# A twelve-layer perceiver: who normalises x at seven layer borders, and when two self attentions' weights are loaded

## Chip, cores and metric

The kernel runs on one core of one Trainium2 chip. The metric is device time in microseconds of one launch; a time "before" is the median of three runs. The profile is one execution more, with its own time. Engines: TensorE (PE in the rows, PEld its weight loads), VectorE (DVE), ScalarE (ACT), GpSimd (POOL) and SyncE (SP), which issues the loads.

## What is computed

x is 64 sequences of 32 tokens of 256 values: 2048 tokens. Twelve layers follow one another, each x = x + layer(layernorm(x)): four blocks L0 to L3, each of a cross attention to a context of 64 x 257 x 256, a self attention over the 32 tokens of a sequence, and an FFN (two of them with a router over experts).

```
x = x + L0_xattn(layernorm(x), ctx, mask, ...)
x = x + L0_attn(layernorm(x), Wq, Wk, Wv, Wo, ...)
x = x + L0_ffn(layernorm(x), ...)
...
x = x + L3_xattn(layernorm(x), ctx, ctx, ...)
x = x + L3_attn(layernorm(x), Wq, Wk, Wv, Wo, bo)
x = x + L3_ffn(layernorm(x), ...)
```

layernorm subtracts the mean of a token's 256 values and divides by the root of their variance + 1e-5. Because a layer adds to x token by token, the last token's sum closes a layer, and the next one's normalisation hangs on it.

## The kernel before

x stays in SBUF as 16 row blocks of 128 tokens (`K.x[:, i, :]`), four blocks to a group. Every layer is a function with one program for each engine; each engine runs its layers one after the other, and semaphores are all that ties the engines together. `barrier` is the wait for the last x of the layer ahead. POOL's program for a norm stands ahead of its `barrier`, so POOL may start on the next layer's norm as soon as it is through with its own work and a group's statistics are there. The other engines wait at the barrier first.

The names that matter. `follow` makes the statistics (mean and variance, `K.mv`) of row block i - 1 on VectorE while block i is added, so the statistics of a layer's last block come last of all. `Norm` (L203) and `NormParts` (L286) are the two forms of the norm, over four groups g = 0 to 3:

- `pool`: the reciprocal root of the variance, `K.rs`, by an add (L245, L330) and a pow (L247, L332); in `NormParts` also `K.nb`, minus mean times root (L333, L335), which ScalarE needs as its bias.
- `apply`: xn = (x - mean) * rs, one instruction of 128x256 for a row block. In `Norm` VectorE does all 16 (L258). In `NormParts` VectorE does two of a group (L343) and ScalarE two (L360).
- `pe`: eight transposes a group, of xn against the identity, into two PSUM banks (L234, L322). All 32 stand ahead of the layer's own products in TensorE's program.
- `evict`: VectorE and ScalarE copy a bank each to `K.xT`. In `NormParts` ScalarE makes an upper part and VectorE subtracts for a lower one (L350), because the products there are made of three partial ones.

`Norm` is used by L0 self attention, L0 FFN, L1 cross attention, L1 FFN, L2 cross attention and L3 cross attention; `NormParts` by L1 self attention, L2 self attention, L2 FFN and L3 self attention.

In L0 self attention (`l0_attn`) POOL clears four `qk` and ten `v` tiles (L1175) behind its norm, and then takes, for each of 16 row blocks, a pow of 128x32 (L1183) for the norm of q and k. The first product is L189 on `l0a_wqk`. Its weights are loaded behind the barrier, 1.3 MB.

In L3 self attention (`wide_attn` with bias False) the four weights are loaded behind the barrier as well. ScalarE and VectorE split each into an upper and a lower part (`upper`, `lower`, L1361); the first four halves, those of q and k, stand between the norm's groups in the two engines' programs.

In L3 cross attention (`l3_xattn`) 64 batches run through `ticks`. For each, POOL subtracts for the context's lower part (L3944) and scales one of four blocks of probabilities (L3976). SP loads the context of a batch, four buffers ahead.

L0 FFN and L1 FFN collect their sums in DRAM and load x back at their end, so at the border behind them all of x comes at about one time.

## Times and profile before

| | us |
|---|---|
| median of three runs | 3618.52 |
| lowest, highest | 3613.38, 3622.97 |
| the profiled execution | 3626.44 |
| its span in the profile | 3624.7 |
| TensorE busy | 3287.8 (91%) |
| VectorE busy | 2199.3 (61%) |
| ScalarE busy | 1308.9 (36%) |
| POOL busy | 1138.8 (31%) |

Shares are of the span. The mean granted clock of TensorE was 0.945 of full speed. A row of the timeline gives start, length, engine, line, operation, what is written from what, and how many instructions of one kind stand together; square brackets hold the idle time of the engine ahead of it and who ended it. Times count from the start of the span.

### The profile page before, as it was taken

To read this page: it belongs to the slowest core of one execution; us is meant where nothing else is said; L and a number is where in the kernel's file an instruction comes from. 1 tells how busy PE (TensorE), PEld (TensorE's weight loads), DVE (VectorE), ACT (ScalarE), POOL (GpSimd) and SP (SyncE) were. 2 spreads that over 40 slices of the span, in tenths; PEclk is the share of its full clock that TensorE was granted. 3 is DMA by queue.
4 is the path that set the end of the run, shared out by engine and by line. 5 is a ranking of instruction groups with operands and counts; after the bars stand their busy time and mean duration, and the time that the engine had idled before them with its cause. 6 is when DMAs were issued, how large, how long until landed. Compare 5 with 4: busy or idle time off the path is not lost.

```text
span 3624.7 us, 95053 instructions
## 1 busy us (share of the span) xinstructions
PE 3287.8 (91%) x40252; PEld 2747.2 (76%) x40252; DVE 2199.3 (61%) x5264; ACT 1308.9 (36%) x3221; POOL 1138.8 (31%) x1717
## 2 busy tenths in 40 slices
PE   7989659988997979999999779979999999998996
PEld 5866547547986758888888667778888878887894
DVE  5757643356665156666666577755444458887557
ACT  5643101333211224444444443323222236665221
POOL 6767124122003334333333343300000025554102
PEclk9999769999996979999999999989999999999997
DMA  5620348541003321111111100012112211111000
GB/s 161 199 68 4 107 164 263 158 147 49 3 19 113 89 76 54 48 48 48 48 48 42 57 2 3 3 48 90 58 60 92 64 42 49 51 50 63 3 3 27
DMA packets 211335, 246.66 MB, mean 68 GB/s; under 512 B 19460, under 2 KB 191232, under 8 KB 207968
## 3 DMA queue, kind: packets, MB, share of 16 engines
q1 hardware_dynamic: 203424, 230.34, 20.2%
q0 software_dynamic: 7488, 10.23, 1.6%
q8 instruction: 320, 5.24, 0.6%
q14 instruction: 103, 0.84, 0.1%
HBM read 221.46 MB, written 18.61 MB: 66 GB/s over the span
## 4 chain that ended last, share of the span: by engine, by line
PE 77%; DVE 12%; issue 4%; POOL 3%; ACT 3%; DMA 1%; SPq 0%; ACTq 0%; POOLq 0%; DVEq 0%
PE psum L189 46%; PE psum L3648 11%; PE psum L983 2%; PE psum L3898 2%; PE psum L955 2%; PE psum L3107 1%; PE psum L3208 1%; PE psum L3176 1%; PE psum L3888 1%; PE psum L968 1%; DVE l2a_ss L1651 1%; POOL l0a_ms L1183 1%; DVE g_xn L258 1%; PE psum L3117 1%; DVE g_xn L1658 1%
## 5 line engine op out<-in xcount | busy, mean ns | idle before, releaser
L245 POOL TENSOR_SCALAR g_rs<-g_mv 128x4 f32<-128x4 f32 x24 | 5.1, 213 | 773.9 <-DVE g_mv L378 773.4
L3648 PE MATMUL psum<-l2f_hhi,l2f_whi 128*128 128x512 f32 x512 | 199.3, 389 | 0.0
L3648 PE MATMUL psum<-l2f_hlo,l2f_whi 128*128 128x512 f32 x512 | 199.2, 389 | 0.0
L3648 PE MATMUL psum<-l2f_hhi,l2f_wlo 128*128 128x512 f32 x512 | 199.2, 389 | 0.0
L189 PE MATMUL psum<-l2x_kT,l2x_Qp 128*128 128x257 f32 x768 | 179.0, 382 | 2.7 <-ACT g_xn L3531 2.7
L3702 DVE CAST l2f_hhi<-l2f_tmp 128x512 fp32r<-128x512 f32 x96 | 41.0, 427 | 201.7 <-ACT l2f_tmp L3765 200.6
L189 PEld LDWEIGHTS psum<-l2x_kT,l2x_Qp 128*128 128x128 f32 x768 | 141.9, 191 | 21.9 <-issue 3.3
L389 DVE TENSOR_TENSOR g_x<-g_x,psum 128x256 f32<-128x256 f32 x128 | 53.1, 416 | 129.0 <-PE psum L189 125.8
L3765 ACT ACTIVATE l2f_tmp<-psum,g_cols 128x512 f32<-128x512 f32 x64 | 44.2, 690 | 240.2 <-PE psum L3648 240.2
L3531 ACT ACTIVATE g_xn<-psum,l2x_sm 128x257 f32<-128x257 f32 x192 | 89.0, 473 | 90.5 <-DVE l2x_sm L3437 90.5
L4095 ACT ACTIVATE l3x_P<-psum,l3x_sm 128x257 f32<-128x257 f32 x256 | 117.8, 480 | 2.8 <-DVE l3x_sm L4017 2.6
L3648 PEld LDWEIGHTS psum<-l2f_hlo,l2f_whi 128*128 128x128 f32 x512 | 96.1, 188 | 20.2
L3648 PEld LDWEIGHTS psum<-l2f_hhi,l2f_wlo 128*128 128x128 f32 x512 | 96.1, 188 | 20.0
L3648 PEld LDWEIGHTS psum<-l2f_hhi,l2f_whi 128*128 128x128 f32 x512 | 96.1, 188 | 19.8
L200 ACT ACTIVATE l2x_Pc<-psum 128x384 f32<-128x384 f32 x128 | 61.2, 494 | 134.6 <-PE psum L189 134.5
L189 PE MATMUL psum<-g_xn_parts,l2x_tokhi 128*128 128x384 f32 x256 | 93.7, 366 | 3.5 <-DVE l2x_PTlo L3460 1.7
L3446 DVE TENSOR_SCALAR g_xn<-g_xn,l2x_sm 128x257 f32<-128x257 f32 x192 | 91.6, 532 | 2.3
L3460 DVE SCALAR_TENSOR_TENSOR l2x_PTlo<-psum,l1f_next_rk,g_xn_parts 128x384 fp32r<-128x384 f32 x128 | 73.1, 613 | 32.1 <-ACT g_xn_parts L3541 31.3
L1592 POOL TENSOR_TENSOR l2a_ss<-l2a_ss,g_negh 128x32 f32<-128x32 f32 x16 | 90.8, 5673 | 1.3
L3107 PE MATMUL psum<-l1f_next_GG,l2x_cT 128*128 128x257 f32 x256 | 81.6, 401 | 8.4 <-ACT l2x_Qp L200 5.6
L1183 POOL TENSOR_TENSOR l0a_ms<-l0a_ms,g_negh 128x32 f32<-128x32 f32 x16 | 86.8, 5428 | 1.3
L189 PE MATMUL psum<-l2x_PTlo,l2x_tokhi 128*128 128x384 f32 x256 | 86.4, 337 | 0.0
(877 smaller groups left out, 10770.2 us busy)
## 6 DMA issues: line engine op xcount, KB each, us to landing
l2f_raw<-L2f_h SPq DMA_DIRECT2D x64, 512.0 KB, 3.4
l0f_w<-L0f_w SPq DMA_DIRECT2D x23, 1024.0 KB, 8.0
l0x_ctxT<-ctxT SPq DMA_DIRECT2D x64, 257.0 KB, 2.8
l1x_ctxT<-ctxT SPq DMA_DIRECT2D x64, 257.0 KB, 6.3
l0x_ctok<-ctx SPq DMA_DIRECT2D x64, 256.0 KB, 3.1
l1x_ctok<-ctx SPq DMA_DIRECT2D x64, 256.0 KB
l2x_cT<-ctxT SPq DMA_DIRECT2D x64, 256.0 KB, 2.8
l2x_tok<-ctx SPq DMA_DIRECT2D x128, 128.0 KB, 2.9
```

The lines of the kernel that those rows point to most:

```text
L189: ins = e.matmul(out, lhsT, rhs, start=start and n == 0, stop=stop and n == len(pairs) - 1, skip_group_check=skip)
L955: t = e.matmul(self.s_bank[par][32 * j:32 * j + 32, ch * self.nk:(ch + 1) * self.nk], qT[r, ch, 32 * j:32 * j + 32], kT[r, ch, j, :], star ...
L983: t = e.matmul(self.o_bank[j][par * hd:(par + 1) * hd, ch * 32:ch * 32 + 32], v[s, b * hd:(b + 1) * hd], PT[s, par * nch + ch, :], start=n ...
L1183: e.tensor_tensor(m, m, K.negh[:, 0:32], ALU.pow).then_inc(*rs_ok.up())
L1592: e.tensor_tensor(f, f, K.negh[:, 0:32], ALU.pow).then_inc(*rs_ok.up())
L3107: e.matmul(z[:, 0:257], a[:, 1, k], GG[:, 1, :], start=True, stop=False, skip_group_check=True)
L3446: t = e.tensor_scalar(P[b % 3][:, n, :], P[b % 3][:, n, :], m(4)[:, n:n + 1], None, ALU.mult)
L3460: e.scalar_tensor_tensor(out=lo[:, kt, :], in0=banks.of(("T", b, kt))[:, 0:384], scalar=rk[:, b, kt:kt + 1], in1=hi[:, kt, :], op0=ALU.mul ...
L3531: t = e.activation(P[k][:, n, :], bank[n][:, 0:257], ACT.Exp, bias=sm[:, k, 2, n:n + 1], scale=0.125, accum_out=sm[:, k, 3, n:n + 1])
L3648: t = e.matmul(z, a, b, start=c == 0 and u == 0, stop=c == 7 and u == 2)
L3898: t = e.transpose(z[:, r * 128:(r + 1) * 128], P[b % 3][:, r, kt * 128:(kt + 1) * 128], ident[:])
L4095: e.activation(P[k][:, r, :], bank[r][:, 0:257], ACT.Exp, bias=sm[:, k, 1, r:r + 1], accum_out=sm[:, k, 2, r:r + 1]).then_inc(*exps.up())
```

## The change

`Norm` and `NormParts` get an argument `early`. With it, POOL also normalises: all four blocks of groups 0, 1 and 2, each right behind the group's root. It can do so while the layer ahead still runs, since this stands ahead of its barrier. In `Norm` POOL does two blocks of group 3 as well and ScalarE the other two, for which POOL now makes `K.nb`; in `NormParts` group 3 stays with VectorE and ScalarE. VectorE has no `apply` in `Norm` any more.

`early` is on for L0 self attention, L0 FFN, L1 FFN and L3 cross attention (`Norm`), and for L3 self attention (`NormParts`). L1 and L2 cross attention have it off; there POOL does two blocks of each group and ScalarE two, behind the statistics as before. L1 self attention, L2 self attention and L2 FFN are as before.

The weights of L0 self attention are loaded in L0 cross attention (ahead of batch 32), those for q and k of L3 self attention in L3 cross attention (ahead of batch 8). The split of the latter is done there too: ScalarE's four copies at batches 36 to 39, POOL's four subtractions at batches 40 to 43, each at the end of a tick. v and o are loaded and split as before.

Three waits are also eased: the first products of L0 self attention and of L2 cross attention wait for group 2 and not for all four, and the routers' first products for group 1.

```diff
 class Norm:
-    def __init__(self, K, second=None, first=False):
+    def __init__(self, K, second=None, early=True):
...
+    def by_act(self, g):
+        return not self.early or g == 3
+
+    def normed(self, w, g):
+        if self.early:
+            w.wait_ge(self.xn_pool.at(14 if g == 3 else 4 * g + 4))
+        else:
+            w.wait_ge(self.xn_pool.at(2 * g + 2))
+        if self.by_act(g):
+            w.wait_ge(self.xn_act.at(2 if self.early else 2 * g + 2))
...
     def pool(self, e, w):
...
-            e.tensor_tensor(K.rs[:, sl], K.rs[:, sl], K.negh[:, 0:4], ALU.pow).then_inc(*self.rs.up())
+            t = e.tensor_tensor(K.rs[:, sl], K.rs[:, sl], K.negh[:, 0:4], ALU.pow)
+            if self.by_act(g):
+                t.then_inc(*step.up())
+                e.tensor_scalar(K.nb[:, sl], K.mv[:, sl, 0], -1.0, None, ALU.mult).then_inc(*step.up())
+                w.wait_ge(step.now())
+                e.tensor_tensor(K.nb[:, sl], K.nb[:, sl], K.rs[:, sl], ALU.mult).then_inc(*self.rs.up())
+            else:
+                t.then_inc(*self.rs.up())
+            w.wait_ge(self.rs.now())
+            for i in range(4 * g, 4 * g + (2 if self.by_act(g) else 4)):
+                e.tensor_scalar(K.xn[:, i, :], K.x[:, i, :], K.mv[:, i, 0:1], K.rs[:, i:i + 1], ALU.subtract,
+                                ALU.mult).then_inc(*self.xn_pool.up())
...
 class NormParts:
...
     def pool(self, e, w):
...
             e.tensor_tensor(K.nb[:, sl], K.nb[:, sl], K.rs[:, sl], ALU.mult).then_inc(*self.rs.up())
+            if self.ahead(g):
+                for i in range(4 * g, 4 * g + 4):
+                    e.tensor_scalar(K.xn[:, i, :], K.x[:, i, :], K.mv[:, i, 0:1], K.rs[:, i:i + 1], ALU.subtract,
+                                    ALU.mult).then_inc(*self.xn_pool.up())
...
 def l0_xattn(K):
...
             for b in range(4, 64):
+                if b == 32:
+                    K.first.sp(e)
                 fetch(b)
...
 def l0_attn(K):
...
-            load_rows(e, wt, wqk, A["L0a_qk"])
-            load_rows(e, wt, wv, A["L0a_v"])
-            load_rows(e, wt, wo, A["L0a_o"])
...
-                norm.ready(w, i // 4)
-                w.wait_ge(mark["w"])
+                norm.ready(w, max(i // 4, min(i + 2, 3)))
+                w.wait_ge(K.first.w_in.at(0))
...
-            norm.all_ready(w)
...
 def wide_attn(K, pre, bias, eps, scale, keep, brow_name):
...
+        ahead, own = (None, "qkvo") if bias else (K.last, "vo")
...
-            for u in range(6):
+            for u in range(4 if ahead else 0, 6):
...
+        def in_norm(split):
+            return (lambda g: None) if ahead else split
...
-            norm.dve(e, w, lambda g: lower(e, w, g))
+            norm.dve(e, w, in_norm(lambda g: lower(e, w, g)))
...
 class Router:
...
-            self.norm.ready(w, i // 4)
+            self.norm.ready(w, max(i // 4, 1))
...
 def l3_xattn(K):
...
             for b in range(64):
+                if b == 8:
+                    K.last.sp(e)
...
+            def weights(b):
+                if 40 <= b < 44:
+                    K.last.pool(e, b - 40)
...
+            def weights(b):
+                if 36 <= b < 40:
+                    K.last.act(e, b - 36)
```

How instructions stand on three of the places. The names: g_rs, g_nb, g_xn and g_x are the tiles `K.rs`, `K.nb`, `K.xn` and `K.x`; l0a, l1x, l3x and l3a are the layers L0 self attention, L1 cross attention, L3 cross attention and L3 self attention; xn x4 are four instructions.

POOL ahead of L0 self attention, last group, before:

```order
L245 TENSOR_SCALAR g_rs<-g_mv 128x4
L247 TENSOR_TENSOR g_rs<-g_rs,g_negh 128x4
L1175 MEMSET l0a_qk 128x1024 x4
L1175 MEMSET l0a_v 128x512 x10
L1181 TENSOR_SCALAR l0a_ms<-l0a_ms 128x32
```

and with the change, from group 2's steps on:

```order
L271 TENSOR_SCALAR g_xn<-g_x,g_mv,g_rs 128x256 x4
L259 TENSOR_SCALAR g_rs<-g_mv 128x4
L261 TENSOR_TENSOR g_rs<-g_rs,g_negh 128x4
L264 TENSOR_SCALAR g_nb<-g_mv 128x4
L266 TENSOR_TENSOR g_nb<-g_nb,g_rs 128x4
L271 TENSOR_SCALAR g_xn<-g_x,g_mv,g_rs 128x256 x2
L1262 MEMSET l0a_qk 128x1024 x4
L1262 MEMSET l0a_v 128x512 x10
L1268 TENSOR_SCALAR l0a_ms<-l0a_ms 128x32
```

Fourteen steps on g_xn stand now ahead of the memsets, twelve of them ahead of the last group's root.

POOL ahead of L1 cross attention, last group, before:

```order
L1970 DMA acc<-l0f_y,l0f_sidx 4992x256 x7
L166 UNCONDITIONAL_BRANCH
L245 TENSOR_SCALAR g_rs<-g_mv 128x4
L247 TENSOR_TENSOR g_rs<-g_rs,g_negh 128x4
...
L2364 MEMSET l1x_bd 128x128 x2
L2374 COPY l1x_csel<-l1x_ctxT 128x256 x4
```

and with the change:

```order
L2074 DMA acc<-l0f_y,l0f_sidx 4992x256 x7
L166 UNCONDITIONAL_BRANCH
L259 TENSOR_SCALAR g_rs<-g_mv 128x4
L261 TENSOR_TENSOR g_rs<-g_rs,g_negh 128x4
L264 TENSOR_SCALAR g_nb<-g_mv 128x4
L266 TENSOR_TENSOR g_nb<-g_nb,g_rs 128x4
L271 TENSOR_SCALAR g_xn<-g_x,g_mv,g_rs 128x256 x2
...
L2468 MEMSET l1x_bd 128x128 x2
L2478 COPY l1x_csel<-l1x_ctxT 128x256 x4
```

The root of a group has grown from two instructions to four, and two steps on g_xn stand between one group's and the next one's, four times.

ScalarE at the start of L3 self attention, before:

```order
L360 ACTIVATE g_xn<-g_x,g_nb,g_rs 128x256 x6
L200 ACTIVATE g_xT_parts<-psum 128x512 x2
L200 ACTIVATE l3a_wqhi<-l3a_wq 128x2x512
L360 ACTIVATE g_xn<-g_x,g_nb,g_rs 128x256 x2
...
L200 ACTIVATE g_xT_parts<-psum 128x512 x2
L200 ACTIVATE l3a_wkhi<-l3a_wk 128x2x512
```

and with the change:

```order
L200 ACTIVATE g_xT_parts<-psum 128x512 x2
L404 ACTIVATE g_xn<-g_x,g_nb,g_rs 128x256 x2
L200 ACTIVATE g_xT_parts<-psum 128x512 x6
L200 ACTIVATE l3a_q<-psum 128x512
L200 ACTIVATE l3a_wvhi<-l3a_wv 128x512
```

Six of the eight steps on g_xn and the four copies of weights are gone; the two steps of group 3 stand ahead of the copies out of PSUM of groups 1 to 3. VectorE's program there has changed in the same way.

## Rows read from the trace of the kernel before

**Rows 1.** Stretches (L0 cross attention, border to L3 cross attention): us, busy by engine (count), PEclk, DMA share, GB/s.
```profile
70.00:220.00 150.00, 149.39 (x1527) 123.98 (x1525) 109.12 (x411) 103.01 (x425) 112.99 (x281) 1.00 0.62 181
2934.50:2944.30 9.80, 7.65 (x32) 5.35 (x32) 8.97 (x20) 2.46 (x5) 3.96 (x6) 0.65 0.71 221
```

**Rows 2.** Timeline at the border L0 cross to L0 self attention.
```profile
220.38 0.19 POOL L245 TENSOR_SCALAR g_rs<-g_mv 128x4 f32<-128x4 f32 x1
...
233.06 4.79 DVE L258 TENSOR_SCALAR g_xn<-g_x,g_mv,g_rs 128x256 f32<-128x256 f32 x8
...
234.58 4.16 POOL L1175 MEMSET l0a_qk<- 128x1024 f32 x4
...
238.68 5.86 POOL L1175 MEMSET l0a_v<- 128x512 f32 x10
...
245.72 3.75 PE L189 MATMUL psum<-l0a_wqk,g_xT 128*128 128x512 f32 x4 [0.73 <-issue]
...
252.11 5.43 POOL L1183 TENSOR_TENSOR l0a_ms<-l0a_ms,g_negh 128x32 f32<-128x32 f32 x1
```

**Rows 3.** Timeline at the border L0 self attention to L0 FFN.
```profile
414.46 0.26 POOL L245 TENSOR_SCALAR g_rs<-g_mv 128x4 f32<-128x4 f32 x1 [7.48 <-DVE g_mv L378]
...
419.88 1.73 PE L234 MATMUL psum<-g_ident,g_xn 128*128 128x128 f32 x8 [0.16 <-DVE g_xn L258]
```

**Rows 4.** Timeline at the border L1 self attention to L1 FFN.
```profile
1081.35 0.26 POOL L245 TENSOR_SCALAR g_rs<-g_mv 128x4 f32<-128x4 f32 x1 [9.54 <-DVE g_mv L378]
...
1081.70 8.16 PE L234 MATMUL psum<-g_ident,g_xn 128*128 128x128 f32 x32 [1.85 <-DVE g_xn L258]
```

**Rows 5.** Timeline at the border L2 FFN to L3 cross attention.
```profile
2928.53 1.01 POOL L247 TENSOR_TENSOR g_rs<-g_rs,g_negh 128x4 f32<-128x4 f32 x1
...
2934.54 0.26 POOL L245 TENSOR_SCALAR g_rs<-g_mv 128x4 f32<-128x4 f32 x1 [5.00 <-DVE g_mv L378]
...
2944.33 6.25 PE L189 MATMUL psum<-g_xT,l3x_wq 128*128 128x512 f32 x14 [0.73 <-issue]
```

**Rows 6.** Timeline at the border L3 cross to L3 self attention.
```profile
3322.93 0.23 POOL L330 TENSOR_SCALAR g_rs<-g_mv 128x4 f32<-128x4 f32 x1
...
3324.96 0.23 POOL L330 TENSOR_SCALAR g_rs<-g_mv 128x4 f32<-128x4 f32 x1
...
3330.49 2.81 PE L322 MATMUL psum<-g_ident,g_xn 128*128 128x128 f32 x24 [2.13 <-ACT g_xn L360]
...
3334.09 1.07 ACT L360 ACTIVATE g_xn<-g_x,g_nb,g_rs 128x256 f32<-128x256 f32 x2
...
3336.00 1.29 DVE L350 TENSOR_TENSOR g_xn_parts<-psum,g_xT_parts 128x512 fp32r<-128x512 f32 x2
...
3336.14 1.97 PE L322 MATMUL psum<-g_ident,g_xn 128*128 128x128 f32 x8 [2.85 <-DVE g_xn L343]
...
3343.83 0.36 PE L189 MATMUL psum<-g_xT_parts,l3a_wqhi 128*128 128x256 f32 x1 [2.19 <-DVE l3a_q L1387]
```

**Rows 7.** Timeline at the border L0 FFN to L1 cross attention.
```profile
609.22 0.20 POOL L245 TENSOR_SCALAR g_rs<-g_mv 128x4 f32<-128x4 f32 x1 [8.28 <-DVE g_mv L378]
...
622.57 3.69 PE L189 MATMUL psum<-l0f_next_wvc,g_xT 128*128 128x256 f32 x16 [0.73 <-DVE g_xT L265]
```

**Rows 8.** Timeline at the border L1 FFN to L2 cross attention.
```profile
1294.28 0.20 POOL L245 TENSOR_SCALAR g_rs<-g_mv 128x4 f32<-128x4 f32 x1 [8.22 <-DVE g_mv L378]
...
1309.51 2.82 PE L189 MATMUL psum<-l1f_next_wq,g_xT 128*128 128x384 f32 x8 [0.96 <-ACT g_xT L282]
```

**Rows 9.** POOL's groups by line and shape: busy us, mean ns | idle before, releaser.
```profile
L3944 POOL TENSOR_TENSOR l3x_ctxlo<-l3x_ctxT,l3x_ctxhi 128x512 fp32r<-128x512 f32 x64 | 81.6, 1275 | 12.3 <-ACT l3x_ctxhi L200 12.3
...
L3308 POOL TENSOR_SCALAR l1f_next_wk<-l2x_tok,l1f_next_nms,l2x_w 128x256 f32<-128x256 f32 x128 | 72.4, 575 | 11.2 <-POOL l2x_w L3302 11.1
L3976 POOL TENSOR_SCALAR l3x_P<-l3x_P,l3x_sm 128x256 f32<-128x256 f32 x64 | 61.4, 959 | 0.0
...
L3969 POOL TENSOR_TENSOR l3x_tail<-l3x_P,l3x_sm 128x4 f32<-128x4 f32 x64 | 13.0, 204 | 147.2 <-DVE l3x_sm L4022 147.2
```

More of the change, by code:

```diff
@@ L229, in pe @@
         for g in range(4):
+            self.normed(w, g)
             for c in range(2):
@@ L269, in evict, with apply @@
                                 ALU.add).then_inc(*self.dv.up())
-        ticks(4, {0: apply, 1: evict}, [0, 1])
     def act(self, e, w):
         K = self.K
-        for g in range(4):
+        def apply(g):
+            if not self.by_act(g):
+                return
+            w.wait_ge(self.rs.at(g + 1))
+            for i in range(4 * g + 2, 4 * g + 4):
+                e.activation(K.xn[:, i, :], K.x[:, i, :], ACT.Identity, scale=K.rs[:, i:i + 1],
+                             bias=K.nb[:, i:i + 1]).then_inc(*self.xn_act.up())
+        def evict(g):
             w.wait_ge(self.ps.at(2 * g + 2))
@@ L340, in apply @@
         def apply(g):
+            if self.ahead(g):
+                return
             w.wait_ge(self.rs.at(g + 1))
@@ L357, in apply @@
         def apply(g):
+            if self.ahead(g):
+                return
             w.wait_ge(self.rs.at(g + 1))
@@ L407, in l0_xattn @@
     x, xn, xT, mvc, mv, rs = K.x, K.xn, K.xT, K.mvc, K.mv, K.rs
+    K.first = FirstWeights(K)
     with ExitStack() as sc:
@@ L1102, in barrier, with __init__, sp, act @@
         w.wait_ge(K.sig("x").at(0))
+class FirstWeights:
+    def __init__(self, K):
+        self.K, self.scope = K, ExitStack()
+        T = lambda name, shape: K.tile("next_" + name, shape, F32, self.scope)
+        self.wqk, self.wv, self.wo = T("wqk", [128, 2, 512]), T("wv", [128, 2, 256]), T("wo", [128, 4, 256])
+        self.w_in = K.sig("first_w_in", 16, lasting=True)
+    def sp(self, e):
+        A = self.K.A
+        load_rows(e, self.w_in, self.wqk, A["L0a_qk"])
+        load_rows(e, self.w_in, self.wv, A["L0a_v"])
+        load_rows(e, self.w_in, self.wo, A["L0a_o"])
+class LastWeights:
+    def __init__(self, K):
+        self.K, self.scope = K, ExitStack()
+        T = lambda name, shape, dt=F32: K.tile("next_" + name, shape, dt, self.scope)
+        raw = {n: K.shared("next_w" + n, [128, 2, 1024], self.scope) for n in "qk"}
+        self.W = {n: (T(f"w{n}hi", [128, 2, 1024], F32R), raw[n][1]) for n in "qk"}
+        self.raw = {n: raw[n][0] for n in "qk"}
+        S = lambda name, unit=1: K.sig("last_" + name, unit, lasting=True)
+        self.w_in, self.hi_ok, self.lo_ok = S("w_in", 16), S("w_hi"), S("w_lo")
+        self.units = [(n, slice(h * 512, (h + 1) * 512)) for n in "qk" for h in range(2)]
+    def sp(self, e):
+        for n in "qk":
+            load(e, self.w_in, self.raw[n][:], self.K.A["L3a_" + n].rearrange("(c p) m -> p c m", p=128))
+    def act(self, e, u):
+        n, cols = self.units[u]
+        self.K.w(e).wait_ge(self.w_in.now())
+        copy_act(e, self.W[n][0][:, :, cols], self.raw[n][:, :, cols]).then_inc(*self.hi_ok.up())
+    def pool(self, e, u):
+        n, cols = self.units[u]
+        self.K.w(e).wait_ge(self.hi_ok.at(u + 1))
+        e.tensor_tensor(self.W[n][1][:, :, cols], self.raw[n][:, :, cols], self.W[n][0][:, :, cols], ALU.subtract).then_inc(*self.lo_ok.up())
 def l0_attn(K):
@@ L1241, in wide_attn @@
         T = lambda name, shape, dt=F32: K.tile(name, shape, dt, sc)
-        raw = {n: K.shared("w" + n, [128, 2, 1024], sc) for n in "qkvo"}
-        W = {n: (T(f"w{n}hi", [128, 2, 1024], F32R), raw[n][1]) for n in "qkvo"}
-        raw = {n: raw[n][0] for n in "qkvo"}
+        ahead, own = (None, "qkvo") if bias else (K.last, "vo")
+        if ahead:
+            sc.enter_context(ahead.scope)
+        raw = {n: K.shared("w" + n, [128, 2, 1024], sc) for n in own}
+        W = {n: (T(f"w{n}hi", [128, 2, 1024], F32R), raw[n][1]) for n in own}
+        raw = {n: raw[n][0] for n in own}
+        if ahead:
+            W.update(ahead.W)
         wo, bo = raw["o"][:].rearrange("p a (b d) -> p (a b) d", b=4), T("bo", [1, 256])
@@ L3061, in pe @@
             norm.pe(e, w)
-            norm.all_ready(w)
             ahead.ready(w)
@@ L3978, in pool @@
             w.wait_ge(zero.at(4))
-            ticks(64, {0: lower, 1: queries, 3: divide, (3, "bias"): bias}, [3, (3, "bias"), 1, 0])
+            def weights(b):
+                if 40 <= b < 44:
+                    K.last.pool(e, b - 40)
+            ticks(64, {0: lower, 1: queries, 3: divide, (3, "bias"): bias, (3, "w"): weights}, [3, (3, "bias"), 1, 0, (3, "w")])
         def dve(e):
```

70 lines of the change are left out of this document (40 added, 30 removed).

## The prediction, written before the changed kernel ran

> **What bounds the kernel now.** I read the busy time by stretches first. Inside a layer TensorE hardly pauses, 149.39 of 150 us in L0 cross attention; at a border it is busy 7.65 of 9.8 us, and with transposes [rows 1]. The matmul stream inside the layers is not touched, so what can move are the borders. There the next layer starts with 32 transposes of the normalised x, and these wait for a normalisation that starts only when the last row block of x is complete. I then read the timeline at each border [rows 2 to 8] and last the prices of like POOL work [rows 9]. Seven borders change. I call them B1 (L0 cross to L0 self attention), B2 (L0 self attention to L0 FFN), B3 (L1 self attention to L1 FFN), B4 (L2 FFN to L3 cross attention), B5 (L3 cross to L3 self attention), B6 (L0 FFN to L1 cross attention) and B7 (L1 FFN to L2 cross attention). At B1 to B4 POOL takes three of four groups ahead of the border. At B5 it does so too, but replaces work that VectorE and ScalarE shared. At B6 and B7 nothing can be done ahead: x arrives all at once, and POOL and ScalarE take over from VectorE.
>
> **The price that decides.** One normalising step on POOL is a TENSOR_SCALAR of 128x256 with two per-partition scalars, in SBUF. The trace of before has none of g_xn on POOL. The nearest row is L3308, the same form: 575 ns over 128 of them. Another 128x256 TENSOR_SCALAR, L3976, takes 959 ns [rows 9]. The difference is company: L3976 runs each time beside VectorE's own scaling of the same probabilities. That the two engines can hold each other up shows at B1 too, where eight VectorE steps took 4.79 us, 0.60 each, and POOL's memsets ran beside the second half [rows 2]. At the borders VectorE does statistics or reads PSUM when POOL normalises, as beside L3308, so I take 0.58 and keep 0.96 as the other end.
>
> The Trainium skill (SBUF — State Buffer, section Who interferes with whom) says that a VectorE instruction in a 2-port mode or with two SBUF inputs and a GpSimd instruction share one port pair, and that the second to issue blocks fully. By that rule the 0.96 of L3976 is a wait and not POOL's own pace, and here 0.58 would hold wherever VectorE runs no such instruction; the trace agrees as far as the two rows go.
>
> The steps to the reciprocal root (add, pow, and for the bias of ScalarE negate and multiply) take 2.03 us a group, from one L330 to the next [rows 6]; without the bias pair I take 1.4, the pow being 1.01 [rows 5]. Transposes cost 2.81/24 = 0.117 us each [rows 6], eight 0.9. The eight after them took 1.97, about twice as long each, which is the lower of the clock's two levels (1.2 and not 2.4 GHz); at B4 the granted clock was 0.65 over the whole border, a mixture of both [rows 1].
>
> **B1.** POOL is free at 220.38 [rows 2]. Three groups take 3 x 1.4 + 12 x 0.58 = 11.2, so they are done at 231.6, before the border. Group 3 waits for the statistics as now, until about 233.2 (VectorE turns to L258 at 233.06); 2.03 and 2 x 0.58 more put it at 236.4, while ScalarE does its two. But POOL's memsets of the attention tiles stand behind it, 4.16 + 5.86 = 10.0 us: they end at 246.5 where they now end at 244.5. The layer then runs at the pace of POOL's pow, 5.43 each, and the first starts at 252.11. Its inputs would be there 6.4 us after the first product (252.11 - 245.72); the product moves to about 239.2, so they are there at 245.6, and the memsets decide: the small step and the pow start at 246.9. Gain 5.2. TensorE alone would gain 6.5.
> The weights of this layer now come in the middle of L0 cross attention, where the DMA engines are busy 0.62 [rows 1]: 1.3 MB, and the batch loads run four buffers ahead, so taken as free. They gain little of themselves: 1.3 MB started at the border, at a rate like the 221 GB/s of B4, would be there in some 6 us, about when the first product can start.
>
> **B2.** POOL has nothing of its own at the end of the layer, it idled 7.48 us before group 3 [rows 3]; four steps of a group are 2.3, so groups 0 to 2 are hidden, as at B3 with 9.54 [rows 4]. TensorE starts at once on 24 transposes. Group 3: statistics at 414.46, + 2.03 + 1.16 = 417.65, + 8 x 0.117 = 418.6. Now the transposes end at 419.88 + 1.73 = 421.6 [rows 3]. The router's products stand directly behind them. Gain 3.0.
> **B3.** Likewise 1081.35 + 2.03 + 1.16 = 1084.5; eight transposes at the lower clock, as the 1.97 of B5: 1086.5; now 1081.70 + 8.16 = 1089.9 [rows 4]. Gain 3.4.
> **B4.** Group 2's pow starts at 2928.53 and lasts 1.01; four steps put it at 2931.9, before the border. Group 3: 2934.54 + 3.2 = 2937.7, transposes 0.9 to 2.0, ScalarE's copy out about half of the 1.07 that it took for two steps [rows 6]: 2939.2 to 2940.3 for the first product, now at 2944.33 [rows 5]. Gain 4.5. The layer's own weights are still loaded after the border; I take them to land just in time, and if they were late this gain would shrink.
>
> **B5.** Here POOL comes late: it reaches the first group only at 3322.93, behind its own work, and ScalarE and VectorE now do the steps quickly: the 24 transposes are through at 3333.3 [rows 6]. With the change POOL needs 3 x 2.03 + 12 x 0.58 = 13.1 us: group 2 is done at 3336.0, and only then come the 2.03 for group 3: 3338.0. On ScalarE and VectorE the work on groups 1 and 2 stands behind group 3's steps in program order, so then follow: two steps (1.07), the copies of groups 1 to 3 (1.1 each by the same row) and VectorE's three pairs of subtractions of 1.29 [rows 6]; the first of these starts near 3340.1, the last ends at 3344.0, and VectorE's copy that frees the product bank (half of 1.29) at 3344.7. TensorE resumes there now at 3343.83: a loss of 0.9, although the q and k weight splits are gone from this stretch. At 0.96 a step it is 12 x 0.38 = 4.6 more. The splits' absence is the other end: if TensorE could take the bank as soon as its first products are done, some 3.3 after 3340, it would be no loss but a gain of 0.5.
> The splits go to L3 cross attention: four ScalarE copies of about 1.1, four POOL subtractions of 2 x 1.275 = 2.55 (L3944 is half the size). POOL idles 147.2/64 = 2.3 us a batch [rows 9], so each overruns by 0.25. Between 0 and 4 x 2.55, I take 0.5. The 2 MB load comes 28 batches before its first use, so it is hidden.
>
> **B6.** POOL starts at 609.22 and needs per group 2.03 + 1.16 = 3.2, four in a row: 622.0. Then eight transposes 0.9 and a copy 0.6 as above: 623.5, now 622.57 [rows 7]. Loss 1.0. **B7.** The same from 1294.28: 1307.1, transposes, and the first product no longer waits for the last copies out: about 1308.8, now 1309.51 [rows 8]. Gain 0.7.
>
> **What the steps do on their way.** POOL's 12 steps run beside the attention of the layer ahead at B1 to B4 and may hold up a VectorE instruction there; no row shows it. At worst each of the 48 costs the layer what company costs POOL between the two rows of the price, 0.38: 18 us. At best nothing. I take 0.8 in all, near the low end, because POOL's steps fall where the layer ahead runs out and VectorE mostly reads PSUM.
>
> **Sum.** - 5.2 - 3.0 - 3.4 - 4.5 + 0.9 + 1.0 - 0.7 + 0.5 + 0.8 = - 13.6 us. The profiled execution took 3626.4 (its span 3624.7), so 3612.8 in its terms; it ran 7.9 over the median of the runs, 3618.5, and these would go to **3604.9**.
>
> **Rivals.**
> A. POOL's step costs 0.96 everywhere. For: it is what the row of the layer ahead of B5 shows. Against: L3308. B1 - 1.7 (POOL is then done ahead only at 236, and the memsets at 250), B2 - 2.2, B3 - 2.6, B4 - 3.7, B5 + 5.5, B6 + 4.0, B7 + 2.3, the rest + 1.3: + 2.9, so 3621.4, slower than before. The place is B5 and B6, where 12 and 8 steps lie on the path; the sign turns at about 0.89 us a step.
> The Trainium skill (Perfetto Trace Analysis, section Optimizing Scalar/DVE Operations) warns that moving work between VectorE and GpSimd may not help because they share a port; if it did so here it would be this case, with the same time.
> B. The clock. Transposes now come spread out between VectorE's steps. Done in one go from the last x on, a microsecond before POOL's group 3, they are done before group 3 is there. At the lower clock 32 cost 32 x 0.23 = 7.4 us and gate B2 to B4 themselves: the transposes end at 420.9, 1087.8 and 2941.0, which takes away 2.3, 1.3 and 1.5. With them 5.1 us less is gained: 3610.0. For: the clock of 0.65 at B4, the eight slow ones at B5. Against: the 24 at B5 that ran at full clock after a like pause.
> C. More comes than the sum says: VectorE's relief at B5 lets TensorE run on (up to 3), the router's first products at B2 run longer at full clock (1.5), no overrun: 3599.9.
> D. The steps are not ahead at B1 to B4. It would need POOL to be busy there; the rows show it free at 220.38 and 2928.53, so it is no more than 0.02. Each of the four would lose 7 us (12 x 0.58) of what the sum gives it: 3632.7.
>
> **Chances.** The sum 0.48, A 0.16, B 0.20, C 0.14, D 0.02. The range 3597 to 3620 reaches into A, whose mildest forms lie below its end, and past C. A measurement of this kernel tells about 0.3% from no change, 10.9 us: faster needs to be under 3607.7. Of the forecast and its neighbourhood nine tenths lie there, of B a quarter, of C all; A is no change but for a tail. Faster 0.60, same 0.34, slower 0.06.
>
> **What would show it.** In the profile after: the mean of POOL's g_xn line (0.58 or 0.96); the first pow of L0 self attention 5 us after less time from the last x of the layer ahead, with no idle POOL ahead of it; the gap of TensorE at B2 to B4 some 3 to 4.5 us shorter; at B5 the group 3 transposes later by 3 us against the last x, and no weight split behind them; at B6 the first product a microsecond later against the statistics. Wrong would be above all a POOL step over 0.7, or any growth of the attention stages themselves.

## The result, and the profile after

The changed kernel took 3647.58 us (median, 3637.95 to 3651.11) where the kernel before took 3618.52 beside it: ratio 1.0071, 95% interval 1.0051 to 1.009. (A ratio is estimated from all runs of both kernels and so is not exactly the quotient of the two medians, which is 1.0080 here.) The forecast was 3604.9, and the range 3597 to 3620 does not hold the time. The profiled execution took 3651.1 (span 3649.4, mean granted clock 0.939), 24.7 over that of before.

The first row to look for was the price of POOL's step. Groups of POOL in the changed kernel (busy us, mean ns | idle before); the second is the step at the border L3 cross to L3 self attention:

```profile
L271 POOL TENSOR_SCALAR g_xn<-g_x,g_mv,g_rs 128x256 f32<-128x256 f32 x72 | 88.1, 1234 | 2.6
L374 POOL TENSOR_SCALAR g_xn<-g_x,g_mv,g_rs 128x256 f32<-128x256 f32 x12 | 14.6, 1224 | 0.0
```

1.23 us and not the 0.58 taken from L3308, nor the 0.96 of L3976 that was held to be the other end [rows 9]. The instructions hardly differ from each other (1208 to 1410 ns over all 84), whatever VectorE does beside them.

At B1 POOL is therefore late where the forecast had it done ahead. Timeline of the changed kernel, POOL and TensorE (start, duration):

```profile
219.33 5.00 POOL L271 TENSOR_SCALAR g_xn<-g_x,g_mv,g_rs 128x256 f32<-128x256 f32 x4
...
232.17 4.84 POOL L271 TENSOR_SCALAR g_xn<-g_x,g_mv,g_rs 128x256 f32<-128x256 f32 x4
...
241.41 3.63 POOL L1262 MEMSET l0a_qk<- 128x1024 f32 x4
244.98 4.74 POOL L1262 MEMSET l0a_v<- 128x512 f32 x10
...
250.11 5.46 POOL L1270 TENSOR_TENSOR l0a_ms<-l0a_ms,g_negh 128x32 f32<-128x32 f32 x1
```

```profile
237.06 1.97 PE L248 MATMUL psum<-g_ident,g_xn 128*128 128x128 f32 x8 [5.24 <-POOL g_xn L271]
241.53 1.97 PE L248 MATMUL psum<-g_ident,g_xn 128*128 128x128 f32 x8 [2.50 <-POOL g_xn L271]
```

TensorE waits 5.24 us for group 2 and 2.50 for group 3, and the first power step comes at 250.11 where it came at 252.11 [rows 2]. The last statistic came 2.45 earlier in this trace, so the power step is 0.5 later against it, where 5.2 earlier was forecast. At B6 and B7, where nothing is ahead, TensorE waits 2.50 us for POOL ahead of each of the last three groups, and at B5 4.9 us ahead of two of them. TensorE at B6 and then at B5:

```profile
623.14 1.97 PE L248 MATMUL psum<-g_ident,g_xn 128*128 128x128 f32 x8 [2.50 <-POOL g_xn L271]
627.61 1.97 PE L248 MATMUL psum<-g_ident,g_xn 128*128 128x128 f32 x8 [2.50 <-POOL g_xn L271]
630.31 5.90 PE L189 MATMUL psum<-l0f_next_wvc,g_xT 128*128 128x256 f32 x16 [0.73 <-issue]
```

```profile
3352.14 1.97 PE L358 MATMUL psum<-g_ident,g_xn 128*128 128x128 f32 x8 [4.86 <-POOL g_xn L374]
3359.03 1.97 PE L358 MATMUL psum<-g_ident,g_xn 128*128 128x128 f32 x8 [4.91 <-POOL g_xn L374]
```

These answer to [rows 7] and [rows 6]; there the first 24 transposes of B5 run in one go of 2.81. At B4 the end of the transposes did come earlier, but the products behind them run slower than before:

```profile
2954.81 1.09 PE L248 MATMUL psum<-g_ident,g_xn 128*128 128x128 f32 x8 [2.71 <-POOL g_xn L271]
2956.64 16.97 PE L189 MATMUL psum<-g_xT,l3x_wq 128*128 128x512 f32 x32 [0.73 <-DVE g_xT L280]
```

The same 32 products took 13.97 in the kernel before, of which [rows 5] show the first 14.

**Where the time went.** The table has two readings of each border. The first is the time from the last statistic (g_mv) to the first product behind the transposes. The second is the shift: how much later an instruction well inside the next stage starts, against the trace of before, less the same shift ahead of the border. It holds what the first products do too.

| border | forecast | to first product: before, after | shift after |
|---|---|---|---|
| B1 | -5.2 | 12.76, 12.78 | +0.5 |
| B2 | -3.0 | 7.27, 5.63 | +0.3 |
| B3 | -3.4 | 8.58, 5.63 | -4.1 |
| B4 | -4.5 | 10.07, 6.66 | -0.4 |
| B5 | +0.9 | 8.18, 18.85 | +8.5 |
| B6 | +1.0 | 9.18, 16.41 | +9.4 |
| B7 | -0.7 | 10.31, 15.21 | +3.4 |
| sum | -14.9 | | +17.6 |

At B3 the shift runs from the last statistic to the end of the router's 64 products. The other 7.1 of the 24.7 arose inside the layers and in the start (which came 2.5 earlier). How much of such a rest is scatter, further traces of the unchanged kernel had to show (experiment 5).

### The profile page after: what moved, and what is told of

Its sections match the earlier page's. It is cut to its first block, busy times and chain, and to the rows that moved or that the text cites. A ratio compares the mean times of both kernels' runs of the same rounds, so it can differ in the third digit from the quotient of the medians.

```text
span 3649.4 us, 95084 instructions
## 1 busy us (share of the span) xinstructions
PE 3287.2 (90%) x40252; PEld 2752.4 (75%) x40252; DVE 2156.7 (59%) x5158; ACT 1318.0 (36%) x3239; POOL 1253.4 (34%) x1829
## 3 DMA queue, kind: packets, MB, share of 16 engines
q8 instruction: 320, 5.24, 0.6%
## 4 chain that ended last, share of the span: by engine, by line
PE 74%; DVE 10%; issue 6%; POOL 5%; ACT 3%; DMA 1%; SPq 0%; ACTq 0%; POOLq 0%; DVEq 0%
PE psum L189 44%; PE psum L3753 11%; PE psum L1030 2%; PE psum L4006 2%; PE psum L1002 2%; PE psum L3212 1%; PE psum L3313 1%; PE psum L3281 1%; PE psum L3996 1%; PE psum L1015 1%; POOL g_xn L271 1%; DVE l2a_ss L1755 1%; POOL l0a_ms L1270 1%; PE psum L3222 1%; PE psum L641 1%
## 5 line engine op out<-in xcount | busy, mean ns | idle before, releaser
L271 POOL TENSOR_SCALAR g_xn<-g_x,g_mv,g_rs 128x256 f32<-128x256 f32 x72 | 88.1, 1234 | 2.6
```

Of the source, the lines that this page charges most:

```text
L271: e.tensor_scalar(K.xn[:, i, :], K.x[:, i, :], K.mv[:, i, 0:1], K.rs[:, i:i + 1], ALU.subtract, ALU.mult).then_inc(*self.xn_pool.up())
```

## The experiments

All ratios are to the kernel before, run on the same chip beside the variant. "Run 2" below is the kernel of experiment 2, and so on. Where two variants are compared, the intervals of both ratios count: together they leave some 9 to 11 us either way.

**1. The forms of POOL's instruction.** The stretch behind the last layer reads (x is the input, p and q are per-partition scalars, and each line stands for one instruction that waits for the one ahead):

```
for _ in range(6):
    form(p, q, ALU.subtract, ALU.mult)
    form(p, q, ALU.add, ALU.mult)
    form(p, q, ALU.mult, ALU.add)
    form(p, q, ALU.mult, ALU.subtract)
    form(p, None, ALU.mult)
    ...
    form(2.0, 3.0, ALU.mult, ALU.add)
```

> The kernel before, with a measuring stretch added behind its last layer: POOL runs ten forms of a 128x256 fp32 instruction, six times each, first with VectorE idle, then beside a VectorE that runs one tensor_scalar of 128x256 after the other, then beside one that adds two SBUF operands. Theory F (the form sets the price): subtract then mult takes 1.2 us even with VectorE idle, add then mult (the form of L3308) 0.58, and company changes little. Rival G (company or the place of the operands sets it): with VectorE idle all forms take about 0.6 us, and subtract then mult grows to about 1.2 only beside VectorE. The time itself is longer by the stretch, some 300 us, and says nothing.

POOL's timeline, VectorE idle: subtract-mult, add-mult, mult-add, mult-subtract, mult alone, add alone, and two immediates:

```profile
3632.07 1.22 POOL L4290 TENSOR_SCALAR l3f_p<-l3f_p,g_mv,g_rs 128x256 f32<-128x256 f32 x1
3633.39 0.55 POOL L4290 TENSOR_SCALAR l3f_p<-l3f_p,g_mv,g_rs 128x256 f32<-128x256 f32 x1
3634.04 0.55 POOL L4290 TENSOR_SCALAR l3f_p<-l3f_p,g_mv,g_rs 128x256 f32<-128x256 f32 x1
3634.69 1.23 POOL L4290 TENSOR_SCALAR l3f_p<-l3f_p,g_mv,g_rs 128x256 f32<-128x256 f32 x1
3636.02 0.92 POOL L4290 TENSOR_SCALAR l3f_p<-l3f_p,g_mv 128x256 f32<-128x256 f32 x1
3637.04 0.92 POOL L4290 TENSOR_SCALAR l3f_p<-l3f_p,g_mv 128x256 f32<-128x256 f32 x1
...
3639.07 0.40 POOL L4290 TENSOR_SCALAR l3f_p<-l3f_p 128x256 f32<-128x256 f32 x1
```

The same instructions beside a VectorE that does one tensor_scalar after the other (first row: add-mult), and beside one that adds two SBUF operands (subtract-mult, add-mult, and last add-mult with each row read in two halves, as L3308 reads it):

```profile
3688.63 0.55 POOL L4290 TENSOR_SCALAR l3f_p<-l3f_p,g_mv,g_rs 128x256 f32<-128x256 f32 x1
...
3763.14 1.28 POOL L4290 TENSOR_SCALAR l3f_p<-l3f_p,g_mv,g_rs 128x256 f32<-128x256 f32 x1
3764.53 0.83 POOL L4290 TENSOR_SCALAR l3f_p<-l3f_p,g_mv,g_rs 128x256 f32<-128x256 f32 x1
...
3771.53 0.59 POOL L4290 TENSOR_SCALAR l3f_p<-l3f_p,g_mv,g_rs 128x256 f32<-128x256 f32 x1
```

Theory F holds. The form sets the price: 1.22 for subtract with mult in either order (from here on the dear form), 0.55 for add and mult in either order (the cheap form), 0.92 for a single operation with a scalar from memory. The last is the form of L3976, whose 0.959 was no company but nearly its own pace. A VectorE with one SBUF operand does not change POOL's price; one with two adds 0.05 to most forms, but 0.28 to add-mult and 0.29 to mult alone (1.21).

VectorE pays as well, in both cases. Its tensor_scalar beside POOL, then the same one after POOL had finished:

```profile
3680.82 0.61 DVE L4327 TENSOR_SCALAR l3f_d<-l3f_d,g_mv,g_rs 128x256 f32<-128x256 f32 x1
...
3744.99 0.41 DVE L4327 TENSOR_SCALAR l3f_d<-l3f_d,g_mv,g_rs 128x256 f32<-128x256 f32 x1
```

It takes 0.41 alone and 0.53 on the mean beside POOL (0.41 to 0.65); the add of two operands takes 0.43 alone and 0.53 beside POOL (up to 0.66).

**2. The same kernel with the cheap form.** The negated mean is made once for each group of four.

```
-  e.tensor_scalar(K.xn[:, i, :], K.x[:, i, :], K.mv[:, i, 0:1], K.rs[:, i:i + 1], ALU.subtract, ALU.mult)
+  e.tensor_scalar(K.nm[:, sl], K.mv[:, sl, 0], -1.0, None, ALU.mult)
+  e.tensor_scalar(K.xn[:, i, :], K.x[:, i, :], K.nm[:, i:i + 1], K.rs[:, i:i + 1], ALU.add, ALU.mult)
```

> The changed kernel with POOL's step written as (x + (-mean)) * rs, add then mult; one more small POOL instruction (0.24 us) makes the negated mean in 12 of 24 groups. Theory F: the step falls from 1.23 to about 0.58 us, and with it the changed kernel comes to what the sum of the prediction gave for that price, 3604.9 against the 3618.5 of before, at most 4 more for the small instructions: 3605 to 3609. Rival H (the place costs too, POOL's steps stand ahead of its own power steps in L0 self attention and ahead of everything at L0 FFN to L1 cross attention and L3 cross to L3 self attention): only part comes back, 3612 to 3622. Theory G of the first run: the step stays near 1.2 and the time near 3647.

Measured: ratio 0.9962 (0.9943 to 0.9982), 3612.75 beside 3626.51. That is 13.8 us less than before, and 1.09% or 39 us less than the change as it was made. POOL's group and TensorE at B4:

```profile
L267 POOL TENSOR_SCALAR g_xn<-g_x,g_nm,g_rs 128x256 f32<-128x256 f32 x72 | 41.2, 582 | 1.3
```

```profile
2918.03 2.84 PE L248 MATMUL psum<-g_ident,g_xn 128*128 128x128 f32 x24 [0.97 <-DVE g_x L429]
2922.08 1.06 PE L248 MATMUL psum<-g_ident,g_xn 128*128 128x128 f32 x8 [1.21 <-ACT g_xn L290]
2924.68 15.67 PE L189 MATMUL psum<-g_xT,l3x_wq 128*128 128x512 f32 x32 [1.54 <-DMA l3x_am<-pairmask]
```

24 transposes run ahead of group 3 in one go, and group 3 waits 1.21 us and not 2.71. The last line shows what comes late next at B4: the layer's own loads. Theory F is confirmed against H. (The absolute 3612.75 would lie in H's range, but the kernel before took 3626.51 there and not 3618.5; as ratios, F foresaw 0.9963 to 0.9974 and H 0.9982 to 1.001.) The borders did not come out term by term (below).

**3 and 4. Two borders set back, one border set back.** In the first, VectorE normalises all groups at B6 and B7 again; in the second, VectorE and ScalarE take two steps of each group at B5 again, with the q and k weights still ahead:

```
     def by_act(self, g):
-        return not self.early or g == 3
+        return self.early and g == 3
...
     def dve(self, e, w):
+        def apply(g):
+            if self.early:
+                return
+            w.wait_ge(self.rs.at(g + 1))
+            for i in range(4 * g, 4 * g + 4):
+                e.tensor_scalar(K.xn[:, i, :], K.x[:, i, :], K.mv[:, i, 0:1], K.rs[:, i:i + 1], ALU.subtract, ALU.mult)
```

```
-                         early=not bias)
+                         early=False)
```

> The changed kernel with the borders L0 FFN to L1 cross attention and L1 FFN to L2 cross attention set back: there VectorE normalises all four groups as in the kernel before. By the two traces these borders took 9.4 and 3.6 us more: if that is the borders' own cost the time falls by 13, to about 3634.5. Rival: the loss at the second one is recovered or lost again in the layers behind, as the shift in L2 self attention moved by itself between 9.7 and 15.8; then it falls by 9 only, to about 3638.

> The changed kernel with the border L3 cross to L3 self attention set back in its normalisation alone: VectorE and ScalarE take two steps each of every group, POOL none; the q and k weights still come and are split during L3 cross attention. Theory I (POOL's twelve steps on the path are the cost there, and having the weights is worth something): 8.1 us less than the changed kernel plus 1 to 3 for the splits that are gone from the border, so 9 to 11 less, 3637 to 3639. Rival J (the absent splits are worth nothing, since the border waits for the normalised x alone): 8 less, 3639.5.

Measured: 1.0043 (1.0026 to 1.006) and 1.005 (1.0033 to 1.0066), so 10 and 8 us less than the change. By the shifts of the traces B6 fell from +9.4 to +0.3 and B7 from +3.4 to -3.3, which is 16. B5 went from +8.5 to -3.8, which speaks for theory I: the absent splits are worth 3.8 if x comes in time. The medians give back less than the shifts (8 us is rival J's number), and the intervals decide neither between 9 and 13 nor between I and J.

**5. The kernel before, once more.**

> The kernel before, unchanged, for a second trace of it. It shows which differences between traces are scatter: the steps of 2 us in L0 FFN, 3 us into L1 self attention and 2 to 4 us inside L2 self attention, which came in some of the variants and not in others. If they are scatter, this trace differs from the first one by some of them (1 to 4 us each) and the borders agree within 0.5 us; if they were effects of the change, all of it agrees within 0.5 us.

Its profiled execution took 3633.9, 7.4 over the first. The borders agree within 0.4 us, but for B7 at 0.8. Of the 7.4, 3.2 lie in the second half of L0 self attention and 3.6 in L2 self attention. So a shift inside these two layers is scatter up to 3 or 4 us, and the traces cannot tell a cost of that size there.

There is a third trace of the same twelve layers: in experiment 1 all that was added stands behind the last one. Its start came 2.3 us earlier, its L0 self attention lasted 3.5 longer, and six borders agree with the first trace within 0.3. At B3 it came 4.4 earlier, since the 64 products of L1's router ran faster (before, then experiment 1):

```profile
1089.66 13.66 PE L189 MATMUL psum<-l1f_wg,g_xT 128*128 128x8 f32 x64
```

```profile
1090.50 9.82 PE L189 MATMUL psum<-l1f_wg,g_xT 128*128 128x8 f32 x64
```

In the first trace the clock was granted at 0.50 for the whole run of products; in this one it was at 0.92 over the first 5 us and at 0.50 from then on. So a gain or loss of up to 4.4 us at B3 is scatter as well, and so is the earlier start. The -4.1 of the table shows nothing beyond the 2.95 by which the first product came earlier.

**6. The weights alone.** With the edits of 3 and 4, and for all `Norm`:

```
-    def __init__(self, K, second=None, early=True):
+    def __init__(self, K, second=None, early=False):
```

> The weights alone: every normalisation as in the kernel before (VectorE at six borders, VectorE and ScalarE at the seventh), the two self attentions' weights during the layer ahead, and the later waits for the last group of the normalised x. Theory I: the border L3 cross to L3 self attention gains 3.8 as in the run before, L1 FFN to L2 cross attention 3.3 from the later wait, L0 cross to L0 self attention at most 1: 7 to 8 less than the kernel before, ratio 0.998. Rival K: the weights bring nothing where x comes late, so only the 3.3 remain, ratio 0.999, and L0 self attention starts as before.

Measured: 0.9975 (0.9961 to 0.9989), 9 us less. Shifts: B1 -2.1, B5 -4.8, B7 -3.2, B3 -3.1, B2 and B4 within 0.6, and B6 +2.2, where 16 products took 5.36 and not 3.69. That fits theory I (0.998); rival K's 0.999 lies just outside the interval. The gain at B7 is that of the later wait: the first product there no longer waits for the last copies. B3 gained too, where only the router's wait differs: its first products wait for the copies of group 1, which is later than before (group 0) and not earlier. Its 64 products took 11.90 there and 13.66 before, inside the 9.82 to 13.66 of the unchanged kernel, so this gain cannot be told from scatter.

**7. What the runs favour.** POOL's cheap step at B1 to B4, VectorE at B6 and B7, VectorE and ScalarE at B5, both sets of weights ahead.

> Everything that the runs so far favour: POOL's step as add then mult at the four borders where it runs ahead, VectorE's steps at L0 FFN to L1 cross attention and L1 FFN to L2 cross attention, VectorE and ScalarE at L3 cross to L3 self attention, both sets of weights ahead. By the shifts of the runs before: the add form's 0.9962, less 2.6 and 5.0 us: ratio 0.9941, about 21 us less than the kernel before. Rival (the clock gives gains back in the layer behind, as in L0 self attention and L3 cross attention): half of the 7.6 is lost, ratio 0.9952 or more.

Measured: 0.9938 (0.9915 to 0.9961), 3602.41 beside 3627.59. This version beats both kernels; the interval holds the expected 0.9941 and the rival's 0.9952. TensorE at B5, to set beside [rows 6]:

```profile
3318.48 2.81 PE L369 MATMUL psum<-g_ident,g_xn 128*128 128x128 f32 x24 [2.13 <-ACT g_xn L415]
3322.48 1.09 PE L369 MATMUL psum<-g_ident,g_xn 128*128 128x128 f32 x8 [1.19 <-DVE g_xn L396]
...
3326.77 0.39 PE L189 MATMUL psum<-g_xT_parts,l3x_next_wqhi 128*128 128x256 f32 x1 [0.33 <-DVE l3a_q L1502]
```

The wait for group 3 is 1.19 us and not 2.85, since no weight split stands ahead of it, and the wait for VectorE's copy is 0.33 and not 2.19.

**8. TensorE kept at work in its pauses.**

```
+                if g == 3:
+                    for _ in range(10):
+                        e.transpose(K.bank[6][:, 0:128], K.xn[:, 0, 0:128], K.ident[:])
```

> The run above with TensorE kept at work in its pauses: ten transposes that nobody reads ahead of group 3 at the four borders, twelve more while L3 cross attention's first products wait. Theory C (the slow level comes after the pause and falls on the products): the 32 products of L3 cross attention take 14.0 us as in the kernel before, not the 15.7 to 17.0 that they took, with a granted clock of 1.00; 2 to 5 us less than the run above, ratio 0.993. Rival L (the slow level comes whatever TensorE does in the pause): the 32 products stay at 15.7 or more and the time is that of the run above, or up to 2 more for the extra transposes.

Measured: 0.9936 (0.9915 to 0.9957), no difference from the version without. Stretches of TensorE from the first product at B4 (us, busy by engine, then the granted clock, DMA share, GB/s), of the change, then of this run:

```profile
2956.60:2961.60 5.00, 4.96 (x6) 2.19 (x7) 0.75 (x1) 0.97 (x2) 2.72 (x4) 0.50 0.17 56
2961.60:2966.60 5.00, 5.00 (x12) 2.07 (x11) 0.75 (x1) 0.69 (x1) 0.00 (x0) 0.89 0.00 0
```

```profile
2927.30:2932.30 5.00, 5.00 (x14) 2.25 (x13) 0.75 (x1) 1.18 (x2) 2.49 (x2) 1.00 0.33 109
```

In the change the first 5 us run at 0.50, the lower of the two levels (1.2 GHz), behind a pause of 2.71 and one of 0.73. The 32 products took 16.97 and 16.97, 15.71 and 15.48 in the four kernels with the dear step, whose pause is that long. They took 15.67 once and 13.97 three times in those with the cheap step and without filling, 13.90 with it. So the longer pause brought the lower level each time and the shorter one once in four; this run was set beside one that had no slow products, and the expected gain could not show. Theory C is not refuted and not shown. Nor is a pause all there is to it: at B6 the 16 products took 5.3 to 5.4 in runs 6, 7 and 11 and 3.7 in the unchanged kernel and runs 3, 8, 9 and 10, with VectorE normalising there and a pause of 0.73 ahead of them in all of these.

**9 to 11. One border, two borders, one form.** From the version of 7: B1 back to VectorE; B2 and B3 back to VectorE; the dear form again.

In L0 self attention, then in L0 FFN and L1 FFN, then in the POOL step:

```
-        norm = Norm(K)
+        norm = Norm(K, early=False)
```

```
-        norm = Norm(K)
+        norm = Norm(K, early=False)
...
-        norm, mark = Norm(K), {}
+        norm, mark = Norm(K, early=False), {}
```

```
-  e.tensor_scalar(K.xn[:, i, :], K.x[:, i, :], K.nm[:, i:i + 1], K.rs[:, i:i + 1], ALU.add, ALU.mult)
+  e.tensor_scalar(K.xn[:, i, :], K.x[:, i, :], K.mv[:, i, 0:1], K.rs[:, i:i + 1], ALU.subtract, ALU.mult)
```

> The best version so far (e5_best, 22 us under the kernel before) with the border L0 cross to L0 self attention alone set back: there VectorE normalises all four groups, while the other three borders keep POOL's steps. Theory M (L0 self attention gives the head start back): it starts 7 us later than in e5_best, but its stretch from start to last x is shorter by 4 to 6, and the time is e5_best's plus 1 to 3, ratio 0.994 to 0.9946. Rival N (the head start is kept, the longer stretch is scatter): plus 7, ratio 0.9957.

> e5_best with the borders L0 self attention to L0 FFN and L1 self attention to L1 FFN set back to VectorE, so that POOL has no normalising steps beside those two attentions. Theory O (POOL's steps cost the attentions beside them some 2 us each): the borders lose 3.0 and 4.3, and the two attentions gain 4 together, so e5_best plus 3, ratio 0.9946. Rival P (the steps cost nothing there): plus 7.3, ratio 0.9958.

> e5_best with one thing set back: POOL's step at the four borders is again subtract then mult, 1.23 and not 0.58 us. The rows of the two traces give the first product behind the last statistics 8.5 later at the first border, 1.4 at the second and third and 0.7 at the fourth: 12 in all, ratio 0.9971. Theory Q (the twelve steps of each border cost the layer ahead as well, since they take POOL 14.8 instead of 7.0 us): 3 to 6 more, ratio 0.998 to 0.9988. Rival: the slack of L0 self attention swallows most of the 8.5: 5 in all, ratio 0.9952.

Measured: 0.9952 (0.9934 to 0.9971), 0.996 (0.9944 to 0.9975), 0.9985 (0.9971 to 0.9999), against 0.9938. B1 is worth 5 us by the medians, between M and N; the intervals hold both, and also no gain at all. In the traces I compare how long L0 self attention lasted, from 280 us of the first trace to its last x. In the four kernels that start it 7.4 early it lasted 5.3 to 8.5 longer than there, on the mean 7.2. Where VectorE normalises at B1 (the unchanged kernel three times, runs 6 and 9) it was 0 to 5.7, on the mean 2.9. So more than half of the head start is missing at the layer's end. But the four with the dear step, which have no head start, lasted 4.3 to 9.0 longer, on the mean 6.5. So theory M, that the head start is given back, is not shown: the longer layer goes with POOL normalising at B1, early or not. Where in the layer it goes is not pinned down; one variant with the early start (run 2) has its stretch of 284 to 292 us at a granted clock of 0.50, the trace of before at 0.79.

B2 and B3 are worth 8 by the medians, the number of rival P; the interval of run 10 holds O's 0.9946 too. The traces speak for P: L0 self attention lasted 7.3 longer without POOL's cheap steps beside it (run 10) and 7.9 with them (run 7), so they cost it nothing that shows.

The form alone is worth 17, give or take 10, where POOL runs ahead at four borders. Expected were 12 from the first products, and 3 to 6 more by theory Q. By the shifts the four borders lost 8.4, 4.4, 3.9 and 2.7, which is 19 already, so the surplus, if there is one, is in what stands behind the first products and not in the layer ahead. The routers' 64 products took 13.66 and 12.98 for 11.35 and 10.37, the 32 at B4 15.48 for 13.97.

## Why the prediction was wrong, step by step

**What bounds the kernel.** Right: in every variant the time moved at the borders.

**The price that decides.** This is the step that failed, and the forecast had named "a POOL step over 0.7" as its sign. "The nearest row is L3308, the same form: 575 ns" is wrong in "the same form": L3308 adds and multiplies, the new instruction subtracts and multiplies. A row of the profile shows operation class, shape and operands, but not the two arithmetic operations; the code does, and the first experiment gives 0.55 and 1.22 for them with nothing beside POOL. The second half of the step failed with it: the 0.959 of L3976 was explained by company and so taken as the upper end, while a single operation with a scalar from memory takes 0.92 alone. The pair of rows was two forms, not one form with and without company, and no upper end had been shown. Given the price that was assumed, the total came out: the cheap form gave 0.9962 (0.9943 to 0.9982), and 3604.9 / 3618.52 is 0.9962. That it agrees so closely is in part luck. The interval is 7 us either way, and the borders of run 2 add up to -18.6 where -14.9 was forecast, with the difference lost inside the layers.

By the forecast's own slope (16.5 us between the sum and rival A, over 0.38 us a step, so 43.4 us per us), 1.23 a step gives -13.6 + 43.4 x 0.65 = +14.6. Measured were +24.7 in the trace. Rival A had the place of the loss, B5 and B6, and the right side of its point at 0.89; it erred in taking 0.96 for the worst, and in its reason, company.

**The Trainium skill's port rule** (SBUF — State Buffer, section Who interferes with whom) that was to explain L3976: it says that a VectorE instruction with two SBUF inputs contends with a GpSimd instruction that reads SBUF, and that one with a single input does not, outside the 2-port modes. For POOL's price the first experiment agrees with both halves (0.55 beside the one, 0.59 to 0.83 beside the other). For VectorE's own price it does not: the tensor_scalar with one input rose from 0.41 to 0.53 on the mean. No row shows whether that instruction ran in a 2-port mode, so whether it is an exception stays open. The rule does not explain the row that it was used for. What the prediction read from the rows of B1, that the two engines hold each other up, was right: VectorE's step took 0.60 there and 0.41 alone, and POOL's memsets took 10.0 beside such steps and 8.4 without them. The other rule cited, that an exchange between VectorE and GpSimd may not help since they share a port (Perfetto Trace Analysis, section Optimizing Scalar/DVE Operations), had the outcome right, but in these runs the port was not the reason: the same exchange with the cheap form gained.

**The terms,** at the cheap step (shift at each border in run 2; in run 7 in brackets):

- B1: -7.4 (-7.4), forecast -5.2. The mechanism is right: POOL's memsets decide. They took 3.62 + 4.72 = 8.3 and not 10.0; it was 9.9 to 10.0 in the five traces in which VectorE normalises beside them and 8.3 to 8.4 in the other eight. The layer itself then lasted some 4 us longer than where VectorE normalises (runs 9 to 11), which the forecast had not. With the dear step the gain was none.
- B2: -2.7 (-2.5), forecast -3.0. The first product came at 4.25 instead of 7.27 after the last statistic, the 3.0 of the forecast. With the dear step 5.63.
- B3: -7.4 (-7.6), forecast -3.4. The first product came 4.3 earlier; the rest is the router's 64 products, 10.58 us for 13.66, with the granted clock at 0.84 over their first 5 us and 0.50 behind. Since the unchanged kernel has 9.82 once, the rest cannot be credited to the change.
- B4: -2.4 (-4.6), forecast -4.5. The first product came 4.1 and 4.6 earlier. In run 2 the products then took 1.7 longer. The loads came nearly in time: 1.54 us of waiting for them, some 0.8 more than the 0.73 that the pause lasts where the copy alone is waited for.
- B5: +1.3, forecast +0.9; with the dear step +8.5, where 0.9 + 12 x 0.65 gives 8.7. Undone, -3.4 to -4.8 in seven kernels: VectorE and ScalarE normalise, and the weights' absence counts.
- B6: +3.0, forecast +1.0. The first product came exactly 1.0 later (10.18 for 9.18), and its 16 products took 5.28 and not 3.69, as they also did in some variants with VectorE at this border (experiment 8). With the dear step 7.2 later (1.0 + 8 x 0.65 = 6.2) and 5.90.
- B7: -3.0, forecast -0.7. The step away from VectorE brought nothing, since VectorE alone does as well (-3.3 in run 3); the later wait brought it, and it was priced too low.
- The L3x splits: 0.5 forecast, and the layer's second half shifted by -0.5 to +1.2 in the variants, so nothing can be told. What POOL's steps do on their way: 0.8 forecast, no cost shown with the cheap step.

**Rival B** was right that the clock takes part of the gains, in another place. The transposes ran at full clock (24 in 2.84); it is the products behind them that ran at the lower level for longer, 3.0 us more at B4, 2.2 at B6 and, at L0's router, 12.77 for 10.83. These 7.1 us are of the size of the 10 that the slope leaves open, but that they are its cause is not shown. Clear of scatter are two of them: L0's router took 12.6 to 13.7 in the four traces with the dear step and 10.6 to 11.7 in the nine others; the products at B4 took 15.5 to 17.0 and, but for run 2, 13.9 to 14.0. **Rival D** held at one border with the dear step: at B1 POOL came to group 2 only at 232.17, after the last x; it put POOL's being busy down as nearly impossible, since the rows show it free, and the steps themselves made it busy. At the other three it fell.

## What to carry to other kernels

Before an operation is moved to another engine at the price of a "like" row, compare the arithmetic operations in the code and not only class, shape and operand count, since a row does not show them; two rows of one class that differ by half are a sign of two forms until something shows otherwise. On POOL write x minus mean, times scale, as x plus the negated mean, times scale. A gain at a border is only had when the first long run of products behind it has been looked at as well: with the pause of 2.7 us of TensorE ahead of it the products at B4 took 1.5 to 3.0 us longer in four traces of four. And one trace of each kernel is not enough to read a border: the same products took 9.82 and 13.66 us in two traces of one kernel.

## What the runs showed of the hardware that was not expected

- POOL's TENSOR_SCALAR of 128x256 fp32 with scalars from memory: 0.55 us for add-mult and mult-add, 1.22 for subtract-mult and mult-subtract, 0.92 for one operation alone (mult, add or subtract), 0.40 for mult-add with two immediates. Add-mult with two scalars is cheaper than either operation alone with one.
- Beside a VectorE with two SBUF operands subtract-mult took 1.28, add-mult 0.83 (0.59 with the rows read in halves), mult-add 0.60 and mult alone 1.21.
- VectorE's tensor_scalar with one tensor operand took 0.41 us alone and 0.41 to 0.65 beside POOL, though POOL lost nothing; its add of two operands 0.43 alone and up to 0.66. Neither engine ever waited for a whole instruction of the other.
- From one execution of the unchanged kernel to the next L0 and L2 self attention differ by 3 to 4 us, and the 64 products of L1's router by 3.8 (9.82 to 13.66), by when the granted clock falls to 0.50.
